# Attention in groups of four row blocks, with the context kept transposed

## The chip, the cores and the metric

The kernel runs on one core of one Trainium2 chip. The metric is the device time of one execution in microseconds (us). Runs of the kernel before took 3472.29, 3473.58 and 3478.68 us; the median is 3473.58 us. The profiled execution took 3475.8 us.

## The reference, cut to what matters

Four layers follow each other on x, of shape (2, 2048, 512). The second is a transformer block with 16 heads of size 32, and the change is in its attention and in the output projection behind it:

```
q, k, v = (x @ Wq + bq), (x @ Wk + bk), (x @ Wv + bv)      # (B, 16, S, 32) each
scores = einsum('bhqd,bhkd->bhqk', q / sqrt(32), k) + attention_bias
scores = where(src_mask, -inf, scores)
probs = softmax(scores, axis=-1)                            # over 2048 keys
ctx = einsum('bhqk,bhkd->bhqd', probs, v)                   # (B, 16, S, 32)
x = x + (ctx.reshape(B, S, 512) @ Wo + bo)
h = layernorm(x) * g2 + beta2
x = x + (gelu2(h @ W1 + b1) @ W2 + b2)
```

The attention bias is an input of 2 x 16 x 2048 x 2048 fp32, 512 MiB, and is read once. Before attention stand an adapter with a layernorm and the projections; behind the block stand a rotation and a gated low-rank response.

## The kernel before, in words

The program has three stages, one block of engine programs each: the embed stage (0 to about 490 us), the attention stage (to about 2495 us) and the feed-forward stage. Every engine's program is written out in order, and semaphores tie them together, so the order of the work is the order of the calls in the loops.

In attention the work is cut into 512 **units**. A unit is 128 query rows against 2048 keys of one head; eight units (RING) share the keys and values of a head, and there are 64 such heads (2 batches, 2 halves of the queries, 16 heads). One unit goes through these steps:

- SyncE (the SP queue) loads 1 MB of bias into `tiles[s]`, one of eight buffers, when the transposes of the unit that had it before are done. Once in eight units it loads keys and queries (`load_kq`) and values (`load_v`), and at the change of a batch or a query half also the eight masks.
- GpSimd (POOL, L1249) adds the mask to the first 1920 columns of the bias. The last 128 columns of the mask are added by TensorE, as a bf16 product with the identity into the scores (L1273).
- TensorE multiplies q and k (`qk`, L1267) into the four banks of `ps_s`, in two halves of two products of 512 columns.
- VectorE (DVE) adds scores and bias and takes the row minimum (`scores`, L1409), half by half; it frees the half for the next unit's product.
- ScalarE (ACT) takes the exponential of 2048 columns and its row sum (`exp`, L1349).
- TensorE transposes the 16 blocks of 128x128 (`transposes`, L1288), four to a chunk, into three banks `ps_p`; ACT (13 of 16 chunks) and DVE (3 of 16) copy the chunks to `p_t` (`take`, L1359 and L1420). A chunk can be transposed when the chunk three before it has been taken.
- After every **pair** of units TensorE multiplies the values by the transposed probabilities (`pv`, L1307): v is the stationary tile, 32 columns wide, so that four products stand side by side in the array. The four are two units times two halves of the keys.
- The two halves have to be summed and transposed back: DVE copies the bank (`parts`, L1444), TensorE transposes it (`parts_rows`, L1315), and DVE takes two reciprocals (L1428) and then scales and adds (`context`, L1430 and L1437) into rows of context. ACT stores the rows once in 16 heads.

In the feed-forward stage eight tiles of 512 rows run through strips of weights ("cards" of 256 KB in a ring of 12). Each tile's context is loaded (one DMA), transposed by TensorE (`ctx_columns`, L1787), copied by ACT (`take_ctx`, L2156) and multiplied by Wo (`out_project`, L1975).

In the rows a tile's name leaves out its number: `at_ps_c` is the bank of PV, `at_ps_p` the three of the transposes, `ff_ctx` the loaded context and `ff_cols` its transpose.

## Time and profile before

| | |
|---|---|
| median of three runs | 3473.58 us |
| profiled execution | 3475.8 us, of which the span of the core is 3474.0 us |
| mean granted TensorE clock | 0.992 of 2.4 GHz |
| busy in the whole span | TensorE 98%, VectorE 67%, ScalarE 66%, GpSimd 69% |
| busy in 1000 to 2000 us, inside attention | TensorE 100%, VectorE 86%, ScalarE 94%, GpSimd 98.7%, DMA 0.90 to 0.91 at 345 GB/s |
| where the stages lie | embed to 490 us, attention to 2495 us, feed-forward to the end |

The table is read by stage: the shares over the whole span mix three stages. In attention three engines are over 90% busy at once. A matmul's end in the profile is modelled and lies beyond the start of the next one, so that the distance from start to start is what a matmul costs, and short pauses do not show as idle time.

### The profile page before, as it was taken

The page shows a single profiled execution, that of the slowest core. Times are in us where ns is not written, and L with a number is a line of the kernel's source. Part 1 is how long each engine was busy: PE and PEld are TensorE (multiplying, and loading weights), DVE is VectorE, ACT ScalarE, POOL GpSimd, SP SyncE. Part 2 cuts the span into 40 slices and gives each one's busy share as a digit, 9 for nine tenths or more (in the row PEclk, how much of TensorE's full clock was granted, in tenths as well). Part 3 has the DMA queues.
Part 4 walks back from the last instruction along what each step waited for, and adds up shares of the span by engine and source line. Part 5 has one row for each costly group of instructions (what it writes and reads, how often), then busy time and mean ns, then how long its engine had stood idle before and what let it go on. Part 6 is the DMA issues. An engine that isn't in the chain of part 4 may idle for free. (4 is left out here: it accounts for less than half of the span.)

```text
span 3474.0 us, 84659 instructions
## 1 busy us (share of the span) xinstructions
PE 3408.8 (98%) x33299; PEld 2692.7 (78%) x33299; DVE 2343.6 (67%) x5039; ACT 2278.9 (66%) x3399; POOL 2395.8 (69%) x942
## 2 busy tenths in 40 slices
PE   7999989999999999999999999999999999999998
PEld 3444448888888888888888888888778888887886
DVE  7776758888888888888888888888623232332333
ACT  2433449999999999999999999999622212221321
POOL 1222249999999999999999999999643324232322
PEclk8999999999999999999999999999999999999998
DMA  6666599888898988898888998888644544564463
GB/s 215 225 235 239 197 367 349 325 337 331 333 401 329 338 331 333 341 389 337 332 332 329 367 370 334 331 327 329 246 144 154 167 137 157 164 191 143 154 210 124
DMA packets 342721, 954.80 MB, mean 275 GB/s; under 512 B 33204, under 2 KB 190004, under 8 KB 267576
## 3 DMA queue, kind: packets, MB, share of 16 engines
q1 hardware_dynamic: 337108, 940.95, 73.4%
q10 hardware_dynamic: 5220, 8.42, 0.6%
q8 instruction: 269, 4.41, 0.5%
q14 instruction: 124, 1.02, 0.1%
HBM read 849.63 MB, written 99.62 MB: 273 GB/s over the span
## 5 line engine op out<-in xcount | busy, mean ns | idle before, releaser
L1249 POOL TENSOR_TENSOR at_tiles<-at_tiles,at_negmask 128x1920 f32<-128x1920 f32 x509 | 1950.7, 3896 | 29.9 <-DMA at_tiles<-in_bias 19.0
L1349 ACT ACTIVATE at_tiles<-at_tiles,at_rmin 128x2048 f32<-128x2048 f32 x512 | 1030.5, 2013 | 2.4 <-DVE at_rmin L1409 2.4
L1288 PE MATMUL at_ps_p<-consts,at_tiles 128*128 128x128 f32 x8192 | 1023.6, 272 | 1.7 <-ACT at_prob_t L1359 1.3
L1288 PEld LDWEIGHTS at_ps_p<-consts,at_tiles 128*128 128x128 f32 x8192 | 936.3, 139 | 72.5 <-DVE at_prob_t L1420 2.0
L1359 ACT ACTIVATE at_prob_t<-at_ps_p 128x512 f32<-128x512 f32 x1664 | 898.2, 603 | 125.0 <-PE at_ps_p L1288 124.9
L1409 DVE CUSTOM_DVE_ANT_0 at_tiles<-at_ps_s,at_tiles,at_rmin 128x1024 f32<-128x1024 f32 x512 | 655.0, 1279 | 171.7 <-PE at_ps_s L1273 171.0
L1267 PE MATMUL at_ps_s<-at_k_stack,at_q_stack 128*128 128x512 f32 x2048 | 700.7, 438 | 8.1 <-DVE at_rmin L1409 6.1
L1409 DVE CUSTOM_DVE_ANT_0 at_tiles<-at_ps_s,at_tiles 128x1024 f32<-128x1024 f32 x512 | 623.9, 1219 | 24.5 <-POOL at_tiles L1249 22.2
L1307 PE MATMUL at_ps_c<-at_prob_t,at_v 128*32 128x128 f32 x16384 | 500.3, 274 | 1.0 <-DVE at_ctx_rows L1437 1.0
L1307 PEld LDWEIGHTS at_ps_c<-at_prob_t,at_v 128*32 128x32 f32 x16384 | 431.6, 110 | 44.2 <-issue 43.0
L1267 PEld LDWEIGHTS at_ps_s<-at_k_stack,at_q_stack 128*128 128x128 f32 x2048 | 310.8, 191 | 62.5 <-issue 51.5
L1420 DVE COPY at_prob_t<-at_ps_p 128x512 f32<-128x512 f32 x384 | 251.9, 683 | 3.0 <-PE at_ps_p L1288 3.0
L1863 PE MATMUL ff_ps_m<-ff_norm_t,ff_w_card 128*128 128x256 f32 x1024 | 234.7, 379 | 1.4 <-ACT ff_feats L2147 0.9
L1863 PEld LDWEIGHTS ff_ps_m<-ff_norm_t,ff_w_card 128*128 128x128 f32 x1024 | 194.2, 190 | 31.1 <-issue 3.3
L2276 POOL TENSOR_TENSOR ff_x<-ff_res,ff_b 128x512 f32<-128x512 f32 x32 | 46.4, 1473 | 229.0 <-DVE ff_x L2447 229.0
L2160 ACT ACTIVATE ff_norm_t<-ff_ps_t,ff_beta_columns,ff_g_columns 128x512 f32<-128x512 f32 (+1 forms) x36 | 23.3, 728 | 255.5 <-PE ff_ps_t L1787 240.2
L633 ACT ACTIVATE em_qk<-em_ps_q,em_bqk 128x512 f32<-128x512 f32 x64 | 44.0, 687 | 190.5 <-PE em_ps_q L446 172.0
L1273 PEld LDWEIGHTS at_ps_s<-at_negmask,ident_bf 128*128 128x128 bf16 x512 | 48.9, 96 | 137.8 <-issue 137.8
L693 POOL TENSOR_TENSOR em_gs_norms<-em_gs_norms,em_half 128x2 f32<-128x2 f32 x32 | 27.9, 871 | 167.1 <-DVE em_gs_norms L747 167.1
L2252 POOL TENSOR_TENSOR ff_hid_sum<-ff_hid_c,ff_hid_d 128x512 f32<-128x512 f32 x32 | 40.6, 1268 | 146.2 <-ACT ff_hid_c L2110 146.2
L2095 ACT ACTIVATE ff_part_m<-ff_ps_m 128x512 f32<-128x512 f32 x32 | 19.1, 597 | 172.9 <-PE ff_ps_m L1863 172.9
L2390 DVE TENSOR_TENSOR ff_hid_c<-ff_ps_m,ff_part_u 128x512 f32<-128x512 f32 x32 | 22.1, 691 | 162.9 <-PE ff_ps_m L1863 162.9
(239 smaller groups left out, 4098.3 us busy)
## 6 DMA issues: line engine op xcount, KB each, us to landing
at_tiles<-in_bias SPq DMA_DIRECT2D x512, 1024.0 KB, 6.3
ff_w_card<-w_mix SPq DMA_DIRECT2D x256, 256.0 KB, 2.7
ff_w_card<-in_W SPq DMA_DIRECT2D x192, 256.0 KB, 2.9
at_k_stack<-k_hi SPq DMA_DIRECT2D x128, 256.0 KB, 5.6
at_k_stack<-k_lo SPq DMA_DIRECT2D x128, 256.0 KB, 5.6
negm<-em_mask_out SPq DMA_DIRECT2D x32, 512.0 KB, 6.5
at_q_stack<-q_hi SPq DMA_DIRECT2D x128, 128.0 KB, 5.3
at_q_stack<-q_lo SPq DMA_DIRECT2D x128, 128.0 KB, 5.3
```

The lines of the kernel that those rows point to most:

```text
L633: act.activation(qk32[:, i % 2, :], ps_q[g % 3][:], ACT.Identity, bias=bqk[:, k, c:c + 1]).then_inc(s_qk32, 1)
L1249: pool.tensor_tensor(tiles[s][:, 0:PCOLS], tiles[s][:, 0:PCOLS], negm[s][:, 0:PCOLS], ALU.add).then_inc(s_pool, 1)
L1267: last = pe.matmul(out, q_st[n % 2][:, s * P:(s + 1) * P], k_st[n % 2][:, c * 512:(c + 1) * 512], start=True, stop=not masked)
L1273: last = pe.matmul(ps_s[:, lo:(c + 1) * 512], net.ident_bf[:], negm[s][:, lo:(c + 1) * 512], start=False, stop=True)
L1288: last = pe.transpose(ps_p[k][:, y * P:(y + 1) * P], tiles[s][:, t * P:(t + 1) * P], ident)
L1307: last = pe.matmul(ps_c[g * HD:(g + 1) * HD, 0:P], v_sb[n % 2][:, t, :], p_t[pr % 2][:, j, t, :], start=(i == 0), stop=(i == QUART - 1))
L1349: act.activation(tiles[s][:, :], tiles[s][:, :], ACT.Exp, bias=rmin[:, s, 1:2], scale=-1.0, accum_out=rsum[:, s:s + 1]).then_inc(s_exp, 1)
L1359: act.activation(p_t[pr % 2][:, j, 4 * c:4 * c + 4, :].rearrange("p t q -> p (t q)"), ps_p[k][:], ACT.Copy).then_inc(s_pe[k], 1)
L1409: v.tensor_tensor_reduce(out=half, in0=ps_s[:, a * HALF:(a + 1) * HALF], in1=half, scale=-1.0, scalar=-MAX_FLOOR if a == 0 else rmin[:, s, ...
L1420: v.tensor_copy(p_t[pr % 2][:, j, 4 * c:4 * c + 4, :].rearrange("p t q -> p (t q)"), ps_p[k][:]).then_inc(s_pe[k], 1)
L1863: last = pe.matmul(bank[:, h * HALF:(h + 1) * HALF], left[:, k, h * P:(h + 1) * P], right[:, k, :], start=(m in (1, 2, 5) and h == 0 and k ...
L2276: pool.tensor_tensor(x2[:, j, :], res[:, j, :], b2, ALU.add).then_inc(s_x2, 1)
```

## The change

PV runs once for a **group** of four units instead of once a pair. Its four products side by side are now the four units, each summed over all 16 key blocks in place, so that nothing is left to add. `p_t` has five buffers of one unit each. The block of PV stands after the next unit's transposes instead of at the end of a pair.

The result of PV is the context transposed (value column down, query across) and stays so. The reciprocals of the row sums have to be turned into that layout: DVE takes the reciprocals of four sums, copies each of them 32 times side by side (`invert`), TensorE transposes this block (`rinv_columns`), DVE copies it out of the bank (`take_rinv`), and one multiplication scales the context (`context`). SyncE stores 64 KB a group.

The output projection takes this layout as it is, so that the feed-forward stage loads the context with 16 DMAs a tile instead of one (`read_ctx`) and has no `ctx_columns` and no `take_ctx` any more. `load_cx` waits for the projection before it (`s_wo`).

The column split of the mask moves from 1920 to 1856 for GpSimd and from 128 to 192 for TensorE. The keys of the head after the next one are loaded behind the bias of the sixth unit, not those of the next one behind the first. The orders of TensorE, ScalarE and VectorE are written anew; ScalarE has two exponentials in a row once in four.

```diff
-    at.pool_columns = S - 128
+    at.pool_columns = S - 192
-    at.p_t = [sb(f"at_prob_t{i}", [P, 2, S // P, P]) for i in range(2)]
+    at.p_t = [sb(f"at_prob_t{i}", [P, S // P, P]) for i in range(4)]
...
+    at.p_t += [sb("at_prob_t4", [P, S // P, P])]
+    at.rinv4 = sb("at_rinv4", [P, 4])
+    at.rinv = sb("at_rinv", [P, 4, HD])
...
+            load_kq(1)
             for n in range(NH):
                 for s in range(RING):
...
                         load_bias((n + 1) * RING + s)
-                        if s == 0:
-                            load_kq(n + 1)
+                        if s == 5 and n + 2 < NH:
+                            load_kq(n + 2)
                         if s == 2:
                             load_v(n + 1)
+                        if s % 4 == 2:
+                            store(2 * n + s // 4 - 1)
...
-                for i in range(QUART):
-                    for g in range(4):
-                        half, j = divmod(g, 2)
-                        t = half * QUART + i
-                        last = pe.matmul(ps_c[g * HD:(g + 1) * HD, 0:P], v_sb[n % 2][:, t, :], p_t[pr % 2][:, j, t, :],
-                                         start=(i == 0), stop=(i == QUART - 1))
+                for t in range(KT):
+                    for j in range(4):
+                        last = pe.matmul(ps_c[j * HD:(j + 1) * HD, 0:P], v_sb[n % 2][:, t, :], p_t[(4 * g + j) % NPT][:, t, :],
+                                         start=(t == 0), stop=(t == KT - 1))
...
+            def rinv_columns(g):
+                pe.wait_ge(s_rv, 2 * g + 2)
+                after(pe, s_cxo, g)
+                pe.transpose(ps_c[:, P:2 * P], rinv[:].rearrange("p j d -> p (j d)"), ident).then_inc(s_rt, 1)
...
+            def invert(g):
+                s = 4 * g % RING
+                dve.wait_ge(s_exp, 4 * g + 4)
+                after(dve, s_rt, g)
+                v.reciprocal(rinv4[:], rsum[:, s:s + 4]).then_inc(s_rv, 1)
+                dve.wait_ge(s_rv, 2 * g + 1)
+                v.tensor_copy(rinv[:], rinv4[:].unsqueeze(2).broadcast_to([P, 4, HD])).then_inc(s_rv, 1)
+
+            def take_rinv(g):
+                dve.wait_ge(s_rt, g + 1)
+                v.tensor_copy(rinv_t[:], ps_c[:, P:2 * P]).then_inc(s_rc, 1)
+
+            def context(g):
+                dve.wait_ge(s_pv, g + 1)
+                dve.wait_ge(s_rc, g + 1)
+                after(dve, s_st[g % 2], 16 * (g // 2))
+                v.tensor_tensor(cx_t[g % 2][:], ps_c[:, 0:P], rinv_t[:], ALU.mult).then_inc(s_cxo, 1)
...
             def load_cx(n):
-                sp.wait_ge(s_ct, 4 * n)
-                sp.dma_start(cx[:], cxv[n]).then_inc(s_cx, 16)
+                sp.wait_ge(s_wo, 4 * n)
+                net.read_ctx(sp, n)
...
             def out_project(n):
+                pe.wait_ge(s_cx, 4 * DC * 16 * (n + 1))
...
-                        last = pe.matmul(ps_m[j][:], t2[:, k, j * P:(j + 1) * P], wo[:, k, :],
+                        last = pe.matmul(ps_m[row_bank(n, j)][:], cx[:, k, j * P:(j + 1) * P], wo[:, k, :],
...
+        def read_ctx(sp, n):
+            for i in range(P // HD):
+                to = net.cx[i * HD:(i + 1) * HD].rearrange("p c (u q) -> p c u q", q=P)
+                for c in range(DC):
+                    sp.dma_start(to[:, c], blocks[i][:, c]).then_inc(net.s_cx, 16)
```

TensorE's program in the middle of attention. Before, a half of four units, from one PV (L1307) to the next; L1267 is a half of `qk`, L1273 the mask, L1288 the transposes, L1315 `parts_rows`:

```order
L1307 MATMUL at_ps_c<-at_prob_t,at_v 32x128 x32
L1267 MATMUL at_ps_s<-at_k_stack,at_q_stack 128x512 x2
L1273 MATMUL at_ps_s<-at_negmask,ident_bf 128x128
L1267 MATMUL at_ps_s<-at_k_stack,at_q_stack 128x512 x2
L1288 MATMUL at_ps_p<-consts,at_tiles 128x128 x12
L1267 MATMUL at_ps_s<-at_k_stack,at_q_stack 128x512 x2
L1273 MATMUL at_ps_s<-at_negmask,ident_bf 128x128
L1315 MATMUL at_ps_c<-consts,at_ctx_parts 128x128
L1288 MATMUL at_ps_p<-consts,at_tiles 128x128 x8
L1267 MATMUL at_ps_s<-at_k_stack,at_q_stack 128x512 x2
L1288 MATMUL at_ps_p<-consts,at_tiles 128x128 x12
L1307 MATMUL at_ps_c<-at_prob_t,at_v 32x128 x32
```

Now, around the one PV (L1320) of four units; L1282 is `qk`, L1288 the mask, L1303 the transposes and L1329 `rinv_columns`:

```order
L1282 MATMUL at_ps_s<-at_k_stack,at_q_stack 128x512 x2
L1303 MATMUL at_ps_p<-consts,at_tiles 128x128 x4
L1320 MATMUL at_ps_c<-at_prob_t,at_v 32x128 x64
L1303 MATMUL at_ps_p<-consts,at_tiles 128x128 x4
L1282 MATMUL at_ps_s<-at_k_stack,at_q_stack 128x512 x2
L1288 MATMUL at_ps_s<-at_negmask,ident_bf 128x192
L1303 MATMUL at_ps_p<-consts,at_tiles 128x128 x8
L1282 MATMUL at_ps_s<-at_k_stack,at_q_stack 128x512 x2
L1303 MATMUL at_ps_p<-consts,at_tiles 128x128 x12
L1282 MATMUL at_ps_s<-at_k_stack,at_q_stack 128x512 x2
L1288 MATMUL at_ps_s<-at_negmask,ident_bf 128x192
L1303 MATMUL at_ps_p<-consts,at_tiles 128x128 x4
```

PV stands between transposes, and every half of `qk` stands alone between transposes, where before two halves followed PV. A group of four has eight such halves, before six places.

VectorE's program around `context`. Before, half of a group (L1409 is `scores` with the reading of its minimum, L1420 `take`, L1444 `parts`, L1428 to L1437 `context`):

```order
L1409 ISA at_tiles,at_rmin<-at_ps_s,at_tiles 128x1024
L1409 ISA at_rmin 128x1
L1420 COPY at_prob_t<-at_ps_p 128x512
L1444 COPY at_ctx_parts<-at_ps_c 128x128
L1409 ISA at_tiles,at_rmin<-at_ps_s,at_tiles,at_rmin 128x1024
L1409 ISA at_rmin 128x1
L1409 ISA at_tiles,at_rmin<-at_ps_s,at_tiles 128x1024
L1409 ISA at_rmin 128x1
L1428 RECIPROCAL at_rinv<-at_rsum 128x2
L1430 TENSOR_TENSOR at_ctx_parts<-at_ps_c,at_rinv 128x64
L1437 SCALAR_TENSOR_TENSOR at_ctx_rows<-at_ps_c,at_rinv,at_ctx_parts 128x32 x2
```

Now, from `take` of the chunk behind PV (L1418) over `invert` (L1427, L1429) and `context` (L1443) on:

```order
L1418 COPY at_prob_t<-at_ps_p 128x512
L1408 ISA at_tiles,at_rmin<-at_ps_s,at_tiles,at_rmin 128x1024
L1408 ISA at_rmin 128x1
L1427 RECIPROCAL at_rinv<-at_rsum 128x4
L1429 COPY at_rinv<-at_rinv 128x128
L1443 TENSOR_TENSOR at_ctx_t<-at_ps_c,at_rinv_t 128x128
L1408 ISA at_tiles,at_rmin<-at_ps_s,at_tiles 128x1024
L1408 ISA at_rmin 128x1
L1408 ISA at_tiles,at_rmin<-at_ps_s,at_tiles,at_rmin 128x1024
L1408 ISA at_rmin 128x1
```

The copy L1429 reads and writes on-chip memory (SBUF); it stands between the reciprocals and the two halves of scores that follow.

TensorE's program in the feed-forward stage, before and now, where the context comes in:

```order
L1912 MATMUL ff_ps_m<-ff_cols,basis 32x128 x16
L1787 MATMUL ff_ps_t<-consts,ff_ctx 128x128 x16
L1975 MATMUL ff_ps_m<-ff_wo,ff_cols 128x512 x16
L1863 MATMUL ff_ps_m<-ff_norm_t,ff_w_card 128x256 x8
```

```order
L1909 MATMUL ff_ps_m<-ff_cols,basis 32x128 x16
L1965 MATMUL ff_ps_m<-ff_wo,ff_ctx 128x512 x16
L1860 MATMUL ff_ps_m<-ff_norm_t,ff_w_card 128x256 x8
```

The 16 transposes of the context are gone in each of the eight tiles; the projection reads the loaded tile.

## Rows read from the trace of the kernel before

**Rows 1.** Busy time in two stretches of attention: PE, PEld, DVE, ACT, POOL, clock, DMA.

```profile
1000.00:1500.00 500.00, 500.00 (x6883) 424.29 (x6885) 429.47 (x940) 470.62 (x678) 493.41 (x129) 1.00 0.91 345
1500.00:2000.00 500.00, 499.99 (x6922) 423.98 (x6923) 428.97 (x933) 470.59 (x677) 493.31 (x129) 1.00 0.90 345
```

**Rows 2.** Timeline of TensorE, one half of a group: start, duration in us, what.

```profile
1499.91 1.95 PE L1307 MATMUL at_ps_c<-at_prob_t,at_v 128*32 128x128 f32 x64
1501.79 0.73 PE L1267 MATMUL at_ps_s<-at_k_stack,at_q_stack 128*128 128x512 f32 x2
...
1502.40 0.71 PE L1267 MATMUL at_ps_s<-at_k_stack,at_q_stack 128*128 128x512 f32 x2
1502.95 1.48 PE L1288 MATMUL at_ps_p<-consts,at_tiles 128*128 128x128 f32 x12
1504.18 0.70 PE L1267 MATMUL at_ps_s<-at_k_stack,at_q_stack 128*128 128x512 f32 x2
...
1504.79 0.28 PE L1315 MATMUL at_ps_c<-consts,at_ctx_parts 128*128 128x128 f32 x1
1504.91 1.04 PE L1288 MATMUL at_ps_p<-consts,at_tiles 128*128 128x128 f32 x8
1505.70 0.71 PE L1267 MATMUL at_ps_s<-at_k_stack,at_q_stack 128*128 128x512 f32 x2
1506.25 1.48 PE L1288 MATMUL at_ps_p<-consts,at_tiles 128*128 128x128 f32 x12
1507.66 1.95 PE L1307 MATMUL at_ps_c<-at_prob_t,at_v 128*32 128x128 f32 x64
```

**Rows 3.** Timeline of VectorE in the same stretch.

```profile
1503.98 1.22 DVE L1409 CUSTOM_DVE_ANT_0 at_tiles<-at_ps_s,at_tiles 128x1024 f32<-128x1024 f32 x1
...
1505.13 0.16 DVE L1428 RECIPROCAL at_rinv<-at_rsum 128x2 f32<-128x2 f32 x1
1505.33 0.23 DVE L1430 TENSOR_TENSOR at_ctx_parts<-at_ps_c,at_rinv 128x64 f32<-128x64 f32 x1
...
1505.98 1.27 DVE L1409 CUSTOM_DVE_ANT_0 at_tiles<-at_ps_s,at_tiles,at_rmin 128x1024 f32<-128x1024 f32 x1
1507.18 0.08 DVE L1409 DVE_READ_ACCUMULATOR2_ANT at_rmin<- 128x1 f32 x1
...
1508.95 1.28 DVE L1420 COPY at_prob_t<-at_ps_p 128x512 f32<-128x512 f32 x2
```

**Rows 4.** L2353 in all (ns min/median/max), and VectorE and GpSimd around its longest.

```profile
L2353 DVE TENSOR_SCALAR ff_norm<-ff_res,ff_mv,ff_rstd x32: 515/518/1483, 2508.4 to 3266.7; 128x512 f32<-128x512 f32 x32
...
2516.48 1.48 DVE L2353 TENSOR_SCALAR ff_norm<-ff_res,ff_mv,ff_rstd 128x512 f32<-128x512 f32 x1 [0.71 <-POOL ff_rstd L2293]
...
2516.41 5.59 POOL L2276 TENSOR_TENSOR ff_x<-ff_res,ff_b 128x512 f32<-128x512 f32 x4
```

**Rows 5.** Timeline of VectorE near the end of embed, copies of one value to 128 places.

```profile
472.38 0.41 DVE L920 COPY rot_c<-em_sins 128x128 f32<-128x128 f32 x2
472.65 0.27 DVE L921 COPY rot_s<-em_sins 128x128 f32<-128x128 f32 x1
```

**Rows 6.** VectorE's reciprocals in attention, all of them (ns min/median/max).

```profile
L1428 DVE RECIPROCAL at_rinv<-at_rsum x256: 158/163/167, 519.4 to 2491.2; 128x2 f32<-128x2 f32 x128
```

**Rows 7.** Bias DMAs issued from 1500 to 1700 us, and SP's queue around a load of keys.

```profile
DMA to landing us min/median/max: 4.7/6.4/12.5
```

```profile
1716.04 0.45 SPq L1104 DMA_DIRECT2D at_k_stack<-k_hi  x1
...
1721.07 2.68 SPq L1099 DMA_DIRECT2D at_tiles<-in_bias  x2
```

**Rows 8.** Feed-forward: busy time as in rows 1, and the first tile's context transposes.

```profile
2513.00:3000.00 487.00, 485.42 (x2294) 403.32 (x2293) 146.11 (x237) 119.97 (x258) 168.77 (x155) 1.00 0.49 155
```

```profile
2495.63 3.65 PE L1787 MATMUL ff_ps_t<-consts,ff_ctx 128*128 128x128 f32 x16 [4.46 <-PEq L1141]
```

**Rows 9.** Who waited for whom, whole run: GpSimd for the bias.

```profile
POOL at_tiles L1249 <- DMA at_tiles<-in_bias: 19.0, 22, 3.7
```

More of the change, by code:

```diff
@@ L1196, in load_v @@
                 _, _, b, qh, h = place(n * RING)
-                after(sp, s_pv, 4 * (n - 1))
+                after(sp, s_pv, 2 * (n - 1))
                 at.read_v(sp, n % 2, b, h)
@@ L1222, in load_ffn, with store @@
                     sp.dma_start(to[:], rows(net.given[a])).then_inc(net.s_ffw, 16)
+            def store(g):
+                if not 0 <= g < NG:
+                    return
+                n, s, b, qh, h = place(4 * g)
+                sp.wait_ge(s_cxo, g + 1)
+                sp.dma_start(net.ctx[(b * QH + qh) * 2 + s // 4, h], cx_t[g % 2][:]).then_inc(s_st[g % 2], 16)
             for u in range(at.early, RING):
@@ L1289, in transposes, with pv @@
                     last.then_inc(s_pt[k], 1)
-            def pv(pr):
-                if not 0 <= pr < NP:
+            def pv(g):
+                if not 0 <= g < NG:
                     return
-                n = pr * 2 // RING
-                after(pe, s_cxo, 2 * pr)
-                if pr % 4 == 0:
+                n = 4 * g // RING
+                pe.wait_ge(s_rc, g + 1)
+                if g % 2 == 0:
                     pe.wait_ge(s_vin[n % 2], 16 * (n // 2 + 1))
-                for u in (2 * pr, 2 * pr + 1):
+                for u in range(4 * g, 4 * g + 4):
                     for c in range(CH):
@@ L1388, in _ @@
                 take(u + 2, 1)
-                store(pr - 3)
-                store(pr - 2)
-            store(NP - 1)
-            for i in range(RING // 2):
-                act.wait_ge(s_st[i], 16 * B * QH)
+                take(u + 2, 2)
+                exp(u + 4)
+                take(u + 3, 0)
+                take(u + 3, 1)
+                take(u + 3, 2)
+                take(u + 3, 3)
+                exp(u + 5)
+                exp(u + 6)
+                take(u + 4, 1)
+                take(u + 4, 2)
+                take(u + 4, 3)
+                exp(u + 7)
+                take(u + 5, 1)
+                take(u + 5, 2)
         @block.vector
@@ L1433, in context @@
-                after(dve, s_st[s // 2], 16 * (n // HEADS))
-                dve.wait_ge(s_rv, 2 * pr + 2)
-                for j in range(2):
-                    own = slice(j * HD, (j + 1) * HD)
-                    v.scalar_tensor_tensor(cx_all[:, s + j, h * HD:(h + 1) * HD], ps_c[:, P + 2 * HD:2 * P][:, own],
-                                           rinv[:, j:j + 1], cx_sb[:, own], ALU.mult, ALU.add).then_inc(s_cxo, 1)
-            def parts(pr):
-                if not 0 <= pr < NP:
-                    return
-                dve.wait_ge(s_pv, pr + 1)
-                v.tensor_copy(cx_sb[:], ps_c[:, 0:P]).then_inc(s_cxs, 1)
@@ L1446, in _ @@
-            for g in range(-1, NU // 4 + 1):
-                u, pr = 4 * g, 2 * g
-                context(pr - 2)
-                scores(u + 3, 1)
-                scores(u + 4, 0)
-                take(u + 1, 0)
-                parts(pr - 1)
-                scores(u + 4, 1)
-                scores(u + 5, 0)
-                context(pr - 1)
-                scores(u + 5, 1)
-                scores(u + 6, 0)
-                take(u + 3, 2)
-                take(u + 3, 0)
-                scores(u + 6, 1)
-                parts(pr)
-                scores(u + 7, 0)
+                s = 4 * g % RING
@@ new lines, in context @@
+            def context(g):
+                if not 0 <= g < NG:
+                    return
+                dve.wait_ge(s_pv, g + 1)
+                dve.wait_ge(s_rc, g + 1)
+                after(dve, s_st[g % 2], 16 * (g // 2))
+                v.tensor_tensor(cx_t[g % 2][:], ps_c[:, 0:P], rinv_t[:], ALU.mult).then_inc(s_cxo, 1)
+            for g in range(-4, NG + 2):
+                u = 4 * g
+                scores(u + 12, 0)
+                take(u + 9, 0)
+                scores(u + 12, 1)
+                invert(g + 2)
+                context(g + 1)
+                scores(u + 13, 0)
+                scores(u + 13, 1)
+                scores(u + 14, 0)
+                take(u + 10, 3)
+                scores(u + 14, 1)
+                take_rinv(g + 2)
+                scores(u + 15, 0)
+                take(u + 12, 0)
+                scores(u + 15, 1)
```

165 lines of the change are left out of this document (54 added, 111 removed).

## The prediction

> **What bounds the kernel now.** I read the busy time by stage first. Inside attention TensorE is busy without a gap, GpSimd 493 of 500 us, ScalarE 471, VectorE 429, and the DMA engines stand at 0.9 [rows 1]. So TensorE sets the pace and GpSimd is close behind it: 129 mask additions take 493 us, 3.82 us each, against 500 / 129 = 3.88 us a unit. Then I read TensorE's timeline from start to start, since ends are modelled. Half a group (two units) goes from 1499.91 to 1507.66, 7.75 us, so that four units take 15.50 us [rows 2]. Attention has 128 groups, 128 x 15.50 = 1984 us, 57% of the span; a microsecond a group is worth 128 us.
>
> **TensorE in attention, part by part** [rows 2]. Eight transposes take 0.79 us in front of a `qk`, twelve take 1.23: 0.11 each, and 0.09 less than 8 x 0.11, because a `qk` that follows transposes starts early. Twelve in front of PV take 1.41, 0.09 more than 12 x 0.11. PV takes 1.88 until the next `qk`.
> - One PV of the double length replaces two. The 32 products stream in 1.70 (1.95 less the 0.27 by which a last matmul's modelled end lies beyond its start), so 0.18 of the 1.88 is the changeover behind it. One changeover in front and one behind go: 0.09 + 0.18 = 0.27 us a group.
> - Eight halves of `qk` follow transposes, before four: 4 x 0.09 = 0.36.
> - `rinv_columns` once replaces `parts_rows` twice: 0.12 (1504.79 to 1504.91).
> - The mask product grows by 64 columns. A masked half takes 0.61 and one without 0.55, so 128 columns cost 0.06, 64 cost 0.03, four units 0.12 more.
>
> The sum is 0.27 + 0.36 + 0.12 - 0.12 = 0.63, so that TensorE alone would need 14.9 us a group. The changeover from PV to transposes isn't in these rows; at 0 it gives 14.7, at twice the 0.18 it gives 15.1; I take 0.18, the row of PV to `qk`.
>
> **The other engines.** GpSimd adds 1856 columns in place of 1920: 3.82 x 64 / 1920 = 0.13 less, 3.70 a unit, 14.8 a group. ScalarE keeps 4 exponentials and 13 chunks, 0.94 x 15.5 = 14.6. VectorE loses two `parts`, two times two scaled additions, and so on, and is off the bound by its total. By totals alone the change would be a gain. What decides is the order on VectorE, where I look at two things.
>
> *The loop through VectorE.* TensorE's chunk (u, 3) in front of PV needs a bank that VectorE takes last in its round; behind PV the chunk (u+1, 0) is what VectorE takes first. From there to the last take VectorE has, start to start [rows 3, 5]: three takes at 0.60 (two last 1.28, one 0.68), three second halves of scores at 1.20, three first halves at 1.15, the reciprocals 0.20, the broadcast copy 0.14, `context` and `take_rinv` about 0.20 each: 9.6 us. TensorE adds a chunk 0.44, PV 3.40 + 0.27, a chunk 0.44: 4.55. Two crossings at 0.2 (estimate, from the 0.28 of a transpose against its slot of 0.12) make 14.6. The loop therefore has about 0.3 us to spare under 14.9, and whatever is put into this stretch of VectorE beyond 0.3 us is added to the group. The 2.5 us in which VectorE is idle lie ahead of the take, waiting for PV, and cannot absorb it.
>
> *The broadcast copy.* L1429 is in this stretch. It reads SBUF and writes SBUF. L920 is the same kind of copy (one value to many places) and goes at 0.14 us for 128 elements (two of them from 472.38 to 472.65) [rows 5]. A take from PSUM costs 0.60 for 512 elements, so that 128 at its rate are 0.13 to 0.15 before any cost of starting an instruction; the SBUF copy leaves no room for one, so it moves its elements faster than a take. Another operation from SBUF to SBUF, L2353, takes 0.52 us as a rule, but 1.48 us once [rows 4]. That time a GpSimd addition had started 0.07 us earlier, and four of those ran back to back for 5.59 us (1.40 each): VectorE's instruction ended shortly after the first of them. So it stood still until GpSimd's instruction was over and then slipped in between two. In attention GpSimd is busy 98.7% of the time with instructions of 3.8 us. The reciprocals, also SBUF to SBUF, never took more than 0.167 us in 256 [rows 6], so not every such operation is held; the copy would be the first in attention that is. Its cost is bounded from both sides: nothing, if it isn't held; up to 3.7 us, the rest of one GpSimd instruction, if it has just missed the gap; and it can't be a gain, as it only adds work.
>
> The Trainium skill ("SBUF — State Buffer", section "Who interferes with whom") speaks against the change here: a copy in a two-port mode shares a port pair with GpSimd, and whichever starts second is blocked for the whole instruction. The Trainium skill ("VectorE: DVE Perf Modes", section "Mode 2×_2P") gives the condition: one source, source and destination in SBUF, outermost dimensions even; the copy of 4 x 32 meets it. By that rule the row of L2353 is no accident, and the reciprocals are free because they are not on the list; the trace agrees with both.
>
> **How long the copy waits.** Spread evenly over 3.7 us it would be 1.85 us, and with 0.1 to get going the group takes 14.6 + 1.95 = 16.5. But the phase isn't free. GpSimd needs 14.8 and gets ahead of a slower TensorE until it waits for its bias. That bias lands 5.0 to 6.4 us after the transposes that free its buffer [rows 7]. Worked from the order, the addition of the third unit of a group then starts some 2.3 us into the group and the next two boundaries are at 6.0 and 9.7; the copy comes at about 8.8, so it waits 0.9 + 0.1 and the group takes 15.6. In every second group eight issues for keys and queries take SP 5.0 us (1716.04 to 1721.07) ahead of that bias, the boundaries move to 7.6 and 11.3, the wait is 2.6 and the group takes 17.2. The mean is 16.4. Earlier or later landings shift this between 15.3 and 16.8. I take 16.2, between the two estimates and the low end: +0.7 x 128 = +90 us.
>
> **Feed-forward.** 16 transposes of context go in each of eight tiles: seven times 16 x 0.11 = 12.3, and 3.4 in the first (its row lasts 3.65, less the 0.27 of a last matmul) [rows 8]: -16 us, since TensorE is busy for 485 of 487 us there [rows 8]. The take of the context by ScalarE falls away beside it. SP has 15 issues more a tile at about 0.45, 7 us; the ring of 12 cards, 8 products of 0.22 us each, is 20 us ahead, so this is hidden, and would cost up to 7 us in a tile were it not. The tail of attention loses one PV and a transposing back, some 1.5 us.
>
> **Sum.** From the profiled execution of 3475.8 us: +90 - 16 - 1.5 = 3548; the median of the runs lies 2 us under the profiled one, so 3546 us.
>
> **The rivals.**
> 1. *The copy is not held.* For it: its source is a value repeated, and only one row shows a copy-like operation held. Then attention goes at 14.9, plus 0.1 for short waits of chunks whose margins I count at 0.1 to 0.2, plus some for GpSimd, whose 19 us of waiting for bias [rows 9] now meet only 0.2 us a group of slack: -0.5 x 128 = -64, with -17.5 and +3: 3395 to 3405, say 3398 us. Chance 0.15.
> 2. *The copy is held, but the engines lock.* If GpSimd's four additions with the copy slipped in need as long as TensorE's 14.9, a longer wait lets GpSimd gain, which brings its boundary forward and shortens the wait. The group then settles at about 15.0 with a wait of 0.3, and is thrown out of it only when masks are loaded. It decides from GpSimd at 14.9 or more a group; my figure is 14.8, so it would drift out, narrowly. -0.5 x 128 + 15 for three losses of about 5 us at new masks - 17.5: 3410 us. Chance 0.17.
> 3. *The main case in a bad phase*, the even spread of 16.5 and the unlucky 16.8: +128 to +166 - 17.5, 3586 to 3625. It is part of the forecast's own range.
>
> **How the numbers follow.** The held copy in drifting phase has 0.68, with 3546 and its own range of 3465 to 3600; below 15.6 us a group it would come out faster than before, which I give 0.05 of the 0.68. Rivals 1 and 2 have 0.32. Faster by over 0.2% is 0.15 + 0.17 + 0.05 = 0.37, within 0.2% (7 us, about what a measurement of this kernel can tell) 0.03, slower 0.60. The range goes down to 3410 to leave out no more than rival 1, and up to 3600.
>
> **What would show it.** In the profile after: L1429 with a mean far over 0.27 us and a maximum near 4 (right), or 0.2 to 0.3 throughout (rival 1). TensorE with idle time of 0.5 to 2 us once a group, released by VectorE's scores or takes, and PV blocks 16.2 us apart; 15.0 apart for either rival, and for rival 2 an L1429 of 0.5 to 0.8 with GpSimd at 99%. The transposes in front of PV 0.09 longer than their slots and PV in 3.6 us show TensorE's own terms. GpSimd's addition gets 0.13 us shorter. The forecast is wrong if L1429 is short, or if it is long while TensorE doesn't wait, which would mean that the loop through VectorE has more room than 0.3 us.

## The result, and the profile after

The changed kernel takes 3721.15 us (median of 4 runs, 3698.09 to 3732.37), the kernel before 3474.62 us: a ratio of 1.070, 95% interval 1.066 to 1.073. The forecast was 3546 us with a range up to 3600: the sign is right, the size under a third of the measured one (+71 in place of +247).

From the page of the profile after: the span, the clock that TensorE was granted in 40 slices (tenths of 2.4 GHz), and the groups of instructions that answer to the terms (busy us, mean ns of one | idle before them, and what ended it).

```profile
span 3723.6 us, 83709 instructions
PEclk8999999999999999999999999999999999999999
L1264 POOL TENSOR_TENSOR at_tiles<-at_tiles,at_negmask 128x1856 f32<-128x1856 f32 x509 | 1889.7, 3746 | 357.3 <-DMA at_tiles<-in_bias 345.0
L1282 PE MATMUL at_ps_s<-at_k_stack,at_q_stack 128*128 128x512 f32 x2048 | 759.9, 453 | 199.0 <-DVE at_rmin L1408 192.4
L1429 DVE COPY at_rinv<-at_rinv 128x128 f32<-128x128 f32 x128 | 266.4, 2081 | 4.4
```

The broadcast copy has a mean of 2.08 us, and TensorE now waits 192 us for VectorE. All instances of the copy (ns min/median/max) show the spread of an instruction that waits:

```profile
L1429 DVE COPY at_rinv<-at_rinv x128: 226/2168/3828, 509.9 to 2749.7; 128x128 f32<-128x128 f32 x128
```

The same stretches of attention as [rows 1], with the same columns:

```profile
1000.00:1500.00 500.00, 449.99 (x5971) 379.75 (x5970) 398.44 (x646) 415.89 (x587) 414.08 (x112) 0.96 0.80 300
1500.00:2000.00 500.00, 454.98 (x6145) 383.13 (x6147) 397.63 (x666) 428.40 (x609) 427.51 (x117) 0.98 0.82 308
```

Every engine does less, and the granted clock (the third column from the end), 1.00 before, is 0.96 and 0.98. The first and last starts of PV's products give the length of attention and, with the span's end, of the rest. After:

```profile
L1320 PE MATMUL at_ps_c<-at_prob_t,at_v x16384: 269/273/298, 521.6 to 2758.5; 128*32 128x128 f32 x200
```

And in the kernel before:

```profile
L1307 PE MATMUL at_ps_c<-at_prob_t,at_v x16384: 272/273/297, 513.3 to 2490.2; 128*32 128x128 f32 x200
```

From the last product to the end it has 3474.0 - 2490.2 = 983.8 us, the changed kernel 3723.6 - 2758.5 = 965.1: feed-forward and the tail gain 18.7 us, where I had 17.5. All the loss is in attention. Taking every PV's first start, 127 groups go from 521.64 to 2755.05, 17.59 us each, where I forecast 16.2 and the kernel before has 15.50 [rows 2].

How a hold looks: VectorE and GpSimd in one group, start and duration.

```profile
1001.81 0.18 DVE L1427 RECIPROCAL at_rinv<-at_rsum 128x4 f32<-128x4 f32 x1
1002.02 3.81 DVE L1429 COPY at_rinv<-at_rinv 128x128 f32<-128x128 f32 x1
1005.74 0.28 DVE L1443 TENSOR_TENSOR at_ctx_t<-at_ps_c,at_rinv_t 128x128 f32<-128x128 f32 x1
...
998.32 7.42 POOL L1264 TENSOR_TENSOR at_tiles<-at_tiles,at_negmask 128x1856 f32<-128x1856 f32 x2
```

GpSimd's second addition had started at 1002.01, 0.01 us before the copy, and ends at 998.32 + 7.42 = 1005.74; the copy ends 0.09 later. Of the 128 copies 116 lasted over 0.4 us, and every one of these ended 0.081 to 0.091 us behind the end of an addition. The rest took 0.23 us or little more.

What it does to TensorE, two groups: in the first the copy took 3.50 us, in the second 2.55.

```profile
1090.83 0.60 PE L1303 MATMUL at_ps_p<-consts,at_tiles 128*128 128x128 f32 x4
1094.25 1.22 PE L1282 MATMUL at_ps_s<-at_k_stack,at_q_stack 128*128 128x512 f32 x2 [2.83 <-DVE at_rmin L1408]
1095.27 0.41 PE L1329 MATMUL at_ps_c<-consts,at_rinv 128*128 128x128 f32 x1
1095.48 1.86 PE L1303 MATMUL at_ps_p<-consts,at_tiles 128*128 128x128 f32 x8
...
1502.79 0.60 PE L1303 MATMUL at_ps_p<-consts,at_tiles 128*128 128x128 f32 x4
1505.24 0.73 PE L1282 MATMUL at_ps_s<-at_k_stack,at_q_stack 128*128 128x512 f32 x2 [1.85 <-DVE at_rmin L1408]
1505.81 0.27 PE L1329 MATMUL at_ps_c<-consts,at_rinv 128*128 128x128 f32 x1
1505.92 1.04 PE L1303 MATMUL at_ps_p<-consts,at_tiles 128*128 128x128 f32 x8
```

Behind 1.85 us of idleness the two products take 0.73 us, behind 2.83 us they take 1.22 and eight transposes 1.86 in place of 1.04. The columns of [rows 1] for the work behind each of the two waits show why: the granted clock is 0.52 in the first and 1.00 in the second.

```profile
1094.20:1097.30 3.10, 3.05 (x12) 2.75 (x13) 2.97 (x5) 0.00 (x0) 3.10 (x2) 0.52 0.98 363
1505.20:1507.30 2.10, 2.06 (x14) 1.66 (x15) 2.08 (x3) 1.11 (x3) 2.10 (x1) 1.00 0.22 90
```

In the first TensorE comes back at the lower of its two levels (1.2 in place of 2.4 GHz). This I had not reckoned with.

**A formula for a group.** With the copy's duration c of each group beside its length, the length less c has a median of 14.97 to 15.03 us in every half-microsecond class of c from 0.5 to 2.5 us, and of 16.1 to 16.2 above that; groups with c under 0.4 mostly take 15.3 to 15.5. Above 2.5 us there are two kinds of group: in the 32 whose work behind the wait was slow the median is 16.2, in the other 21 it is 15.0 as below. So a group takes the larger of 15.3 us (TensorE) and 15.0 + c (the loop through VectorE), and about 1.2 more where the clock fell. In the stretch behind the wait (the next 25 matmuls of TensorE, usually 3.68 us) the groups together take 55 us more than usual. The 32 slow ones have 51 us of it, the cost of the clock in that stretch; the rest are four groups in which TensorE stopped again inside the stretch.

### The profile page after: what moved, and what is told of

It is laid out like the page before. It is cut to its first block and busy times, and to the rows that moved or that the text cites. A ratio compares the mean times of both kernels' runs of the same rounds, so it can differ in the third digit from the quotient of the medians.

```text
span 3723.6 us, 83709 instructions
## 1 busy us (share of the span) xinstructions
PE 3435.5 (92%) x33043; PEld 2702.8 (73%) x33043; DVE 2432.8 (65%) x4271; ACT 2296.7 (62%) x3367; POOL 2334.2 (63%) x942
## 5 line engine op out<-in xcount | busy, mean ns | idle before, releaser
L1264 POOL TENSOR_TENSOR at_tiles<-at_tiles,at_negmask 128x1856 f32<-128x1856 f32 x509 | 1889.7, 3746 | 357.3 <-DMA at_tiles<-in_bias 345.0
L1303 PE MATMUL at_ps_p<-consts,at_tiles 128*128 128x128 f32 x8192 | 1129.1, 279 | 8.1 <-ACT at_tiles L1362 4.6
L1303 PEld LDWEIGHTS at_ps_p<-consts,at_tiles 128*128 128x128 f32 x8192 | 944.2, 143 | 120.1 <-issue 39.1
L1282 PE MATMUL at_ps_s<-at_k_stack,at_q_stack 128*128 128x512 f32 x2048 | 759.9, 453 | 199.0 <-DVE at_rmin L1408 192.4
L1408 DVE CUSTOM_DVE_ANT_0 at_tiles<-at_ps_s,at_tiles 128x1024 f32<-128x1024 f32 x512 | 623.1, 1217 | 22.0 <-POOL at_tiles L1264 15.5
L1418 DVE COPY at_prob_t<-at_ps_p 128x512 f32<-128x512 f32 x384 | 264.4, 688 | 411.1 <-PE at_ps_p L1303 410.5
L1320 PE MATMUL at_ps_c<-at_prob_t,at_v 128*32 128x128 f32 x16384 | 478.0, 273 | 24.5 <-issue 19.2
L1282 PEld LDWEIGHTS at_ps_s<-at_k_stack,at_q_stack 128*128 128x128 f32 x2048 | 322.3, 198 | 231.7 <-DVE at_rmin L1408 222.1
L1320 PEld LDWEIGHTS at_ps_c<-at_prob_t,at_v 128*32 128x32 f32 x16384 | 443.4, 110 | 53.1 <-issue 53.1
L1429 DVE COPY at_rinv<-at_rinv 128x128 f32<-128x128 f32 x128 | 266.4, 2081 | 4.4
L1288 PEld LDWEIGHTS at_ps_s<-at_negmask,ident_bf 128*128 128x128 bf16 x512 | 50.2, 98 | 144.9 <-issue 144.9
L1288 PE MATMUL at_ps_s<-at_negmask,ident_bf 128*128 128x192 bf16 x512 | 134.2, 262 | 0.0
```

The costliest lines, as they stand in the source:

```text
L1264: pool.tensor_tensor(tiles[s][:, 0:PCOLS], tiles[s][:, 0:PCOLS], negm[s][:, 0:PCOLS], ALU.add).then_inc(s_pool, 1)
L1282: last = pe.matmul(out, q_st[n % 2][:, s * P:(s + 1) * P], k_st[n % 2][:, c * 512:(c + 1) * 512], start=True, stop=not masked)
L1288: last = pe.matmul(ps_s[:, lo:(c + 1) * 512], net.ident_bf[:], negm[s][:, lo:(c + 1) * 512], start=False, stop=True)
L1303: last = pe.transpose(ps_p[k][:, y * P:(y + 1) * P], tiles[s][:, t * P:(t + 1) * P], ident)
L1320: last = pe.matmul(ps_c[j * HD:(j + 1) * HD, 0:P], v_sb[n % 2][:, t, :], p_t[(4 * g + j) % NPT][:, t, :], start=(t == 0), stop=(t == KT - 1))
L1408: v.tensor_tensor_reduce(out=half, in0=ps_s[:, a * HALF:(a + 1) * HALF], in1=half, scale=-1.0, scalar=-MAX_FLOOR if a == 0 else rmin[:, s, ...
```

## The experiments

Unless said otherwise the base is the changed kernel. A slot is the time on TensorE from the first start of a step to the next step's; "mean" and "median" are over the 125 whole groups of a trace.

**One reciprocal, no copy.**

```diff
-                v.reciprocal(rinv4[:], rsum[:, s:s + 4]).then_inc(s_rv, 1)
-                dve.wait_ge(s_rv, 2 * g + 1)
-                v.tensor_copy(rinv[:], rinv4[:].unsqueeze(2).broadcast_to([P, 4, HD])).then_inc(s_rv, 1)
+                v.reciprocal(rinv[:], rsum[:, s:s + 4].unsqueeze(2).broadcast_to([P, 4, HD])).then_inc(s_rv, 2)
```

> The changed kernel with the reciprocals written straight into the 128 columns by one instruction, without the broadcast copy. Theory A (the held copy and what it brings about is the whole loss): a group of the changed kernel takes the larger of 15.33 us (TensorE alone) and 15.0 us plus the duration of the copy, and about 1.1 us more where TensorE sat idle over 2.5 us and then started at the lower clock. Without the copy nothing is held, the new reciprocals take 0.2 to 0.3 us, a group takes 15.35 us in place of 17.45, that is 269 us less: 3450 to 3465 us, GpSimd's wait for bias falls back from 345 us to under 40. Rival B (the loss is GpSimd's waiting for its bias, since stores, keys and queries moved on SyncE's queue): the copy gone, still over 3600 us. Rival C (any instruction of that size from SBUF to SBUF is held): the reciprocals of 128 columns have a mean near 2 us and the time stays near 3720 us.

Measured: 3525.47 us, ratio to before 1.016 (1.014 to 1.018). Rivals B and C fall, but theory A's number is missed by 60 us. All reciprocals take the same time, so none is held; but one costs 0.95 us, not 0.2 to 0.3. In the loop it replaces the short reciprocal of 0.17 as well, which makes 15.0 + 0.95 - 0.17 = 15.8 us a group; the median is 15.7 and the mean 16.1. All reciprocals (ns min/median/max):

```profile
L1427 DVE RECIPROCAL at_rinv<-at_rsum x128: 944/949/951, 512.8 to 2564.2; 128x128 f32<-128x128 f32 x128
```

And GpSimd still waited 158 us for its bias, where I expected under 40.

**GpSimd's additions in halves.** Two instructions of 928 columns in place of one of 1856.

> The changed kernel with each GpSimd addition of 1856 columns split in two of 928. Theory A (the copy stands still until the GpSimd instruction under way is over): its mean falls from 2.08 us to 1.0 to 1.2 and its maximum from 3.83 to about 2.1; TensorE never idles over 1.7 us at that place and no masked product behind it runs at the lower clock; a group takes 16.0 to 16.3 us, 3540 to 3580 us in all. Rival (the hold lasts until GpSimd is idle, waiting for bias, or ends by something else than its instruction): mean stays near 2 us or grows, and the time stays at 3700 or more.

Measured: 3702.56 us, ratio 1.064 (1.057 to 1.070). The time speaks for the rival, as does the mean of the copies, 1.93 us where theory A has 1.0 to 1.2; the trace speaks for both. Of 118 held copies 104 ended 0.08 to 0.09 us behind the end of the half under way, as theory A has it, and two at the next. Twelve others did not get in at that boundary and stood through 5 to 7 more halves:

```profile
L1431 DVE COPY at_rinv<-at_rinv x128: 226/709/13706, 509.3 to 2725.7; 128x128 f32<-128x128 f32 x128
```

```profile
625.94 13.32 DVE L1431 COPY at_rinv<-at_rinv 128x128 f32<-128x128 f32 x1
...
614.30 24.88 POOL L1266 TENSOR_TENSOR at_tiles<-at_tiles,at_negmask 128x928 f32<-128x928 f32 x13
```

614.30 + 24.88 = 639.18: the copy ended at 639.26, when GpSimd had run out of biases and stopped. All twelve ended so: GpSimd's next addition came 8.7 us later or more. Such a group took about 30 us, some 13 to 14 more than others; twelve make about 160 us, and without them the kernel would stand at about 3540, the lower end of theory A's range. Why these twelve missed the boundary and the 104 did not is open. The Trainium skill ("SBUF — State Buffer", section "Who interferes with whom") says that the second to start is blocked for the whole of the other's instruction; the 116 holds of the changed kernel agree with that, and the twelve here were longer than it says.

**The reciprocals in PSUM**, so that the copy reads PSUM.

```diff
-                v.reciprocal(rinv4[:], rsum[:, s:s + 4]).then_inc(s_rv, 1)
+                v.reciprocal(ps_c[:, 2 * P:2 * P + 4], rsum[:, s:s + 4]).then_inc(s_rv, 1)
...
-                v.tensor_copy(rinv[:], rinv4[:].unsqueeze(2).broadcast_to([P, 4, HD])).then_inc(s_rv, 1)
+                v.tensor_copy(rinv[:], ps_c[:, 2 * P:2 * P + 4].unsqueeze(2).broadcast_to([P, 4, HD])).then_inc(s_rv, 1)
```

> The changed kernel with the four reciprocals written to PSUM, so that the broadcast copy reads PSUM and writes SBUF; the same two instructions otherwise. Theory A with the condition that both ends lie in SBUF: the copy takes about 0.28 us every time, a group 15.35 us, 3450 to 3470 us. Rival (a copy of this form is held wherever its source is, since its destination is in SBUF): mean near 2 us, time near 3720 us.

Measured: 3503.31 us, ratio 1.009 (1.007 to 1.010). The hold is gone with this one edit, and 218 of the 247 us with it:

```profile
L1429 DVE COPY at_rinv<-at_ps_c x128: 291/292/294, 510.1 to 2528.9; 128x128 f32<-128x128 f32 x128
```

The Trainium skill ("VectorE: DVE Perf Modes", section "Mode 2×_2P") asks for source and destination in SBUF; the trace agrees, 128 times out of 128. The busy time of a stretch:

```profile
1000.00:1500.00 500.00, 485.40 (x6751) 408.70 (x6741) 384.70 (x724) 460.24 (x663) 466.50 (x127) 1.00 0.88 334
```

The clock is back at 1.00. But a group takes 15.8 us, not 15.35, so that 30 us over the kernel before are left. The trace shows three candidates: GpSimd waits for the bias of unit 6 in 49 of 63 rounds of eight (117 of 125 us; unit 6 stands in SyncE's queue behind the eight issues for keys and queries); the four transposes in front of PV take 0.74 us at the median, 0.53 at least; and PV has a mean of 3.82 where its median is 3.63. The next runs take them one by one.

**The kernel before with a copy.**

```diff
...
+                if pr % 2 == 0:
+                    v.tensor_copy(cx_sb[:].rearrange("p (j d) -> p j d", j=2),
+                                  rinv[:].unsqueeze(2).broadcast_to([P, 2, 2 * HD])).then_inc(s_rv, 1)
...
```

> The kernel before with one copy more a group of four units: two reciprocals spread over 128 columns, from SBUF to SBUF, behind the reciprocals of every second pair (its result is overwritten, so that the output stays the same). Theory A (the hold belongs to the copy and to GpSimd's long additions, in whatever order): mean 1.5 to 2.2 us, maximum near 3.9. VectorE has about 1.8 us of short idle stretches a group there, which take part of it: 0.5 to 1.2 us a group, 3540 to 3630 us. Rival (the hold comes from the new order alone, which puts the copy behind the start of an addition): mean under 0.3 us and 3475 to 3480 us.

Measured: 3528.97 us, ratio 1.016 (1.014 to 1.018). Mean 1.44 us, and the 119 held ones end 0.081 to 0.091 behind an addition. The hold does not depend on the new order:

```profile
L1432 DVE COPY at_ctx_parts<-at_rinv x128: 226/1127/3968, 520.9 to 2539.9; 128x128 f32<-128x128 f32 x128
```

128 x 1.44 = 184 us of copies cost 55 us there, 0.3 of their length, since VectorE had room; in the changed kernel every microsecond counts.

**Keys and queries spread.** On the kernel with reciprocals in PSUM: two of the eight issues at each of units 5, 6, 7 and 0.

```diff
...
-                        if s == 5 and n + 2 < NH:
-                            load_kq(n + 2)
+                        if s >= 5 and n + 2 < NH:
+                            load_kq(n + 2, (s - 5,))
+                        if s == 0 and n > 0:
+                            load_kq(n + 1, (3,))
```

> The kernel with the reciprocals in PSUM (no held copy, 3503 us), and the eight issues for keys and queries no longer in a row at unit 5 but two at each of units 5, 6, 7 and 0. There GpSimd waited 117 us for the bias of unit 6 (49 times of 63), which stands behind those eight issues, of 125 us in all. Theory A (the row of eight issues takes GpSimd's lead, and TensorE pays for a part of it): GpSimd's wait falls under 50 us and unit 6 no longer stands out; TensorE gains 15 to 35 us, 3468 to 3488 us. Rival (the bias is late because the bus is full, not because of the issues): the wait stays over 90 us, spread over the units, and the time at 3500 us.

Measured: 3478.18 us, ratio 1.001 (1.000 to 1.002), 25 us less. The time is as expected. GpSimd's wait only fell to 93 us, so that half of the expectation is missed; but it now comes in 111 short pieces, with 15 us at unit 6, and no longer stands out. GpSimd's wait before this edit (us in total, times, longest):

```profile
POOL at_tiles L1264 <- DMA at_tiles<-in_bias: 124.6, 64, 6.8
```

And with it:

```profile
POOL at_tiles L1266 <- DMA at_tiles<-in_bias: 93.4, 111, 3.7
```

**take_rinv behind the last take**, on the same base.

```diff
-                take_rinv(g + 2)
                 scores(u + 15, 0)
                 take(u + 12, 0)
+                take_rinv(g + 2)
```

> The kernel with the reciprocals in PSUM, with take_rinv (0.20 us of VectorE) moved from inside the stretch between the first and the last take of a round to right behind the last take. Theory A (the loop TensorE - VectorE - TensorE through that stretch still binds without the held copy, since the four transposes in front of PV take 0.74 us at the median where the shortest take 0.53): the loop gets 0.2 us shorter, those transposes take 0.53 to 0.6 us, a group 0.15 to 0.2 us less: 3478 to 3485 us. Rival (they wait for something else, such as a take of ScalarE, or PV's instructions): the slot stays at 0.74 and the time at 3500 us.

Measured: 3503.59 us, no change. The slot did fall, from 0.74 to 0.54 us at the median, but the time stayed: GpSimd still waited for its bias (115 us from 600 to 2480 us, where it had been 117), and it is likely that what the loop gave up was waited for there; the pair of edits below bears on it. A miss on the time, and a hit on what those transposes wait for.

**PV in halves**, on the same base, with the next four transposes between the halves.

> The kernel with the reciprocals in PSUM, with the PV of 64 products of a group issued as two halves of 32 and the four transposes that followed it between them. Of its 127 PV blocks ten have a standstill inside and four behind them of up to 3 us, 22 us in all, which no block of 32 products in the kernel before has. Theory A (the long row of short products runs TensorE out of instructions): with halves the standstills of over 0.5 us go, 15 to 22 us less, and two changeovers more cost about 0.25 us a group, 32 us: 3505 to 3520 us in all, with a mean of each half within 0.05 us of its median. Rival (the standstills belong to something else, such as the wait for V or a transfer): they stay, at the same total, and the time is 3530 us or more.

Measured: 3559.28 us, ratio 1.024 (1.023 to 1.026). Standstills inside PV (pauses of over 0.5 us between two of its products) fell from ten to five, 11 to 5 us, and those behind it went; but the transposes now stood half a PV, 1.7 us, earlier in the order and ran into takes that ScalarE had not done. They start 2.33 us behind PV's start, where the first half takes 1.89:

```profile
PEld at_ps_p L1303 <- ACT at_tiles L1370: 67.0, 100, 1.0
...
PE at_ps_p L1303 <- ACT at_prob_t L1379: 44.5, 106, 0.8
```

So the time says nothing of the cause; the experiment was made again in another place, last below. (Rows: who waited for whom, as above, from 600 to 2480 us.)

**Fillers in VectorE's stretch**, on the same base: three, and two, reciprocals of 0.95 us in front of the copy.

> The kernel with the reciprocals in PSUM, with three more instructions of VectorE of 0.95 us each (the reciprocals of 128 columns, written and overwritten) in front of the broadcast copy, about 2.9 us in every group, and nothing held. Theory A (everything put into that stretch lengthens the group by itself, and TensorE starts at its lower clock after an idle stretch of over 2.5 us): TensorE idles 2.6 to 2.9 us once a group, the masked or first products behind it take 1.2 in place of 0.71 us, and a group takes 15.2 + 2.9 + 1.1 = 19.2 us: about 3930 us in all. Rival (the low clock comes from the irregular holds or from elsewhere): 18.1 us a group, 3790 us, and no product of double length behind the gap.

> As the kernel with three instructions of 0.95 us more in VectorE's stretch (which gave 3920 us, 2.58 us of idle TensorE behind which the products took twice as long), but with two of them, 1.9 us a group. Theory A (an idle stretch of 1.6 to 1.9 us does not bring the lower clock, one of 2.6 does): products behind the gap take 0.71 to 0.75 us, a group takes 15.2 + 1.9 = 17.1 to 17.2 us, 3660 to 3690 us. Rival (each idle stretch costs clock in proportion): 17.8 us a group, 3750 us.

Measured (one run each): 3919.64 and 3710.11 us, where theory A has about 3930 and 3660 to 3690. The two fillers, 1.9 us, cost 207 us, 1.62 a group; the third, 0.95 us, costs another 210, 1.64 a group, far over its own length. TensorE with three, in the middle of the run:

```profile
1503.20 0.60 PE L1303 MATMUL at_ps_p<-consts,at_tiles 128*128 128x128 f32 x4
1506.38 0.89 PE L1282 MATMUL at_ps_s<-at_k_stack,at_q_stack 128*128 128x512 f32 x2 [2.58 <-DVE at_rmin L1408]
1507.07 0.41 PE L1329 MATMUL at_ps_c<-consts,at_rinv 128*128 128x128 f32 x1
1507.28 1.91 PE L1303 MATMUL at_ps_p<-consts,at_tiles 128*128 128x128 f32 x8
1508.84 1.20 PE L1282 MATMUL at_ps_s<-at_k_stack,at_q_stack 128*128 128x512 f32 x2
```

The granted clock from 1506.3 to 1509.4 us is 0.58, in the 3.2 us before the wait 1.00. I counted by the time from the start of the last transpose to that of the product which waits. With two fillers it is under 2.0 us in 119 groups of 128, and the work behind it was at full speed in all of them; in the nine longer ones it was slow seven times. With three fillers it is over 2.0 us in 127 groups, and the work was slow in 75. In the changed kernel it was slow behind none of 33 of 1 to 2 us, and behind 32 of 54 longer ones. The low clock thus follows long idle stretches and needs no hold, but not every long one brings it; what decides between them is not shown. The two-filler run came out 20 us above my upper end: I had taken 15.2 us for the base where it was 15.8.

**Both edits**, and then 1920 columns for GpSimd as before.

> The kernel with the reciprocals in PSUM (3503 us), with both the issues for keys and queries spread (which alone gave 3478) and take_rinv behind the last take (which alone shortened the four transposes in front of PV from 0.74 to 0.54 us but left the time at 3503, since GpSimd still waited 115 us for its bias). Theory A (two bounds in a row: the loop of 15.4 us a group and GpSimd's lead; each hides the other): with the lead given back the loop's 0.2 us count, a group takes 15.35 to 15.45 us in the mean in place of 15.58, 3448 to 3462 us, faster than the kernel before. Rival (with the loop shorter GpSimd with its 14.8 us a group has no room left and waits for every bias): the time stays at 3470 to 3480 us and GpSimd waits 120 us or more.

Measured: 3464.60 us, ratio 0.996 (0.995 to 0.998). take_rinv's move, worth nothing alone, is now worth 14 us. 2.6 us above theory A's range; the mean group is 15.5.

> The kernel with both edits, and with 1920 columns added by GpSimd as in the kernel before in place of 1856. TensorE's mask product is 64 columns shorter, 0.12 us a group less; GpSimd needs 4 x 3.85 = 15.4 us a group in place of 14.9. Theory A (GpSimd at 14.9 us stands closely behind TensorE's 15.2): GpSimd becomes the bound, its wait for bias nearly goes, VectorE waits for GpSimd, a group takes 15.5 us: 3465 to 3480 us, slower than with 1856. Rival (TensorE alone decides): 15 us less than with 1856, under 3450 us.

Measured: 3457.82 us, ratio 0.995 (0.994 to 0.997), the lowest median. It came in between: 7 us faster, neither slower nor 15 faster; the two intervals overlap, so that even the 7 us are likely and not sure. TensorE's slots are as before but for the shorter masks. GpSimd's wait for bias is down from 81 to 20 us, and VectorE's wait for GpSimd is up from 19 to 30. From start to start an addition takes 3.83 us, so that GpSimd needs 15.3 of the 15.5 us of a group: it is as near a bound as TensorE, and which of them sets the time is open.

```profile
1000.00:1500.00 500.00, 492.54 (x6851) 416.06 (x6850) 394.43 (x743) 472.18 (x679) 494.56 (x130) 1.00 0.89 346
```

**PV in halves again**, on that fastest version, with a half of scores between.

> The fastest kernel so far (reciprocals in PSUM, issues spread, take_rinv later, 1920 columns: 3458 us) with PV again in two halves of 64 instructions, now with the half of scores that came behind the next transposes between them, whose bank has long been free, so that nothing new is waited for. In the fastest kernel 13 standstills inside PV and 4 behind it make 22 us, and each of those looked up so far ended about 1.2 us behind the landing of a 16 KB load of instructions. Theory A (PV's long row of short products outruns TensorE's instruction loads): with 0.6 us of long products between the halves the standstills fall from 22 us to under 10, while the changeovers add 0.15 to 0.25 us a group (19 to 32 us): 3462 to 3480 us. Rival (the standstills depend only on where in the program a load falls due): they stay at 18 us or more, 3480 to 3492 us.

Measured: 3526.89 us, ratio 1.015 (1.014 to 1.017). Standstills fell from 22 us to 9, as theory A says, and the time was missed by 47: the first transposes behind PV start 4.50 us after PV's start in place of 3.63, so VectorE's first take is later too, and a group takes 16.0 us in the mean in place of 15.5. TensorE waits for VectorE's `at_rmin` 110 times from 600 to 2480 us. That speaks once more for the loop.

## Why the prediction was wrong in size

The mechanism was right: the copy is held, and TensorE waits for it through VectorE. The step that failed is the sum for a group in the held case, 16.2 us where 17.59 were measured: it had the wait of the copy and the loop too short and two terms at nothing. The difference to explain is 1.39 us a group, 176 us.

- **The copy is held** (right). The main case, with its chance of 0.68, is what happened. Neither rival 1 (not held) nor rival 2 (locking) did: c spreads from 0.23 to 3.83 with quartiles 1.12 and 3.08.
- **How long it waits** (too short). The forecast of 16.2 puts 1.74 us on the copy, argued from where the bias lands; measured 2.08, near the even spread of 1.95 that I had as rival 3: 0.34 a group, 43 us. The argument on the phase has waits of 1.0 and 2.6 in turn from group to group; measured are 2.01 and 2.15. GpSimd, with 345 us of waiting for bias against 19 [rows 9], kept no phase.
- **The loop through VectorE** (mis-sized). 14.6 with a copy of 0.14, or 14.46 without, against the measured 15.0: 0.54 a group, 69 us. This is the largest term. In the undisturbed group from 1512.42 the stretch from the first take to the end of the last is 9.9 us with a copy of 0.3, where I had 9.6 with 0.14; PV is 3.64. The rest is the crossings: 1.03 us from the end of the last take's slot (1526.74) to the start of PV (1527.77), and 0.76 from the transposes behind PV (1516.06) to the take (1516.82). I had two chunks of 0.44 and twice 0.2; the crossings are 0.45 each. That estimate was the end of one transpose less its slot; what else a crossing holds no row shows by itself.
- **TensorE alone** (mis-sized, but not on the path). 14.9 forecast; the tenth percentiles of its slots sum to 15.1, and an undisturbed group takes 15.35: twelve transposes with a bank not yet free take 1.29 to 1.38 in place of 1.23, and the four in front of PV 0.67. "0.3 us to spare" was right as a difference, as both sides were low by 0.5.
- **The clock** (missing). 51 us behind the waits, 0.40 a group, no term of the sum.
- **Standstills in PV** (missing). The mean of 3.76 over the median of 3.63 is 0.13 a group, 17 us, while the changeover from PV to transposes is near what I took (3.63 against 3.58).

0.34 + 0.54 + 0.40 + 0.13 = 1.41 against 1.39; that it fits so well is in part luck, as a part of the clock's term is made good before the next PV (a slow group is 1.2 us longer, not 51 / 32 = 1.6). **GpSimd's lead** is inside these: without the hold it was worth 25 us. The prediction used the eight issues in one place for the phase of the additions alone. That they take GpSimd's lead had no price in it, and in the changed kernel 264 of the 345 us of waiting are for the bias of unit 6, behind these issues. **Feed-forward and tail**: 18.7 against 17.5, right. GpSimd's addition: a mean of 3.746 against 3.896 in the page of before, 0.15 less where I had 0.13, right.

With GpSimd's phase unknown, the even spread was the better choice, and the range should have gone past it: every term left out could only add. It stopped at 3600, inside the 3586 to 3625 us of its own rival 3.

## What to carry to other kernels

An instruction of VectorE from SBUF to SBUF beside long GpSimd instructions may cost their length, not its own; look at min/median/max, and move one of its ends to PSUM. A loop between two engines is read from an undisturbed round, start to start, with both ways over the semaphores in it; sums of durations come out short. Where two bounds stand close, remove both before judging either: one edit here gave 0 alone and 14 us with the other.

## What the runs showed of the hardware

- A copy that misses the gap between two GpSimd instructions by 0.01 us waits for the whole next one (3.81 us). With instructions of 1.9 us back to back it sometimes missed several boundaries, up to 13.7 us.
- A reciprocal of 128 columns takes 0.95 us, one of 4 takes 0.17: about 6 ns a column. A copy of 128 from PSUM takes 0.29, a third of the reciprocal.
- TensorE stood still inside or right behind PV 14 times, 22 us, in the kernel with reciprocals in PSUM, never within attention in the kernel before, whose PV is half as long. Each time a load of instructions (16 KB, about 0.9 us) had ended 1.25 to 1.6 us before TensorE went on; such loads come once in 6.6 us (284 from 600 to 2480), so that 14 of 14 so close is hardly chance. One of them on TensorE:

```profile
1458.44 3.70 PE L1320 MATMUL at_ps_c<-at_prob_t,at_v 128*32 128x128 f32 x128
1464.39 0.38 PE L1303 MATMUL at_ps_p<-consts,at_tiles 128*128 128x128 f32 x2 [2.25 <-ACT at_tiles L1362]
```

And the queue of these loads from 1461.5 to 1464.5 (packets, MB, share of 16 engines):

```profile
q8 instruction: 1, 0.02, 2.0%
```

The first view puts the wait down to ScalarE, whose exponential had ended at 1463.6; the load went from 1462.14 to 1463.08. That the long row of short products brings this about is supported by both kernels with halves (22 us down to 9), but neither is clean: both pay for it elsewhere, and in the last one three pauses of about 1 us remain among the transposes, each with a load ended 1.3 to 1.5 us before (the fastest kernel has four of them). So it stays likely and not shown.
